# Mamba and ternary FFN block on eight cores: the tile that holds the scan's states is made bf16 instead of fp32

## The reference, cut to what matters

```python
def step(state, inp):                       # selective scan, one token
    dt_t, u_t, B_t, C_t = inp
    dA = jnp.exp(dt_t[:, :, None] * A[None])
    dBu = (dt_t * u_t)[:, :, None] * B_t[:, None, :]
    state = state * dA + dBu
    y_t = jnp.einsum('bdn,bn->bd', state, C_t)
    return (state, y_t)
...
y = (scan(x) + D[None, :, None] * x) * silu(z)
attn = (y @ _H) @ W_out.T                   # _H: Hadamard, 4096 x 4096
...
h1 = x @ ternary_quant(w1).T ; h3 = x @ ternary_quant(w3).T
ffn = (silu(h1) * h3) @ ternary_quant(w2).T
out = x_in + attn + ffn                     # x = layernorm(x_in) feeds both
```

## Time and profile before

| | us |
|---|---|
| median of 2 runs | 10670.43 (10645.05 to 10695.81) |
| the profiled execution's own time | 10478.75 |
| its span on the slowest core (core 5) | 10476.7 |
| spans of the eight cores | 10430.5 to 10476.7 |
| VectorE busy in that span | 6517.8 (62%) |
| TensorE matmuls busy | 5633.2 (54%) |
| ScalarE busy | 2399.2 (23%) |
| GpSimd busy | 1936.0 (18%) |

### The profile page before, as it was taken

One profiled execution on the slowest core, in us unless ns is written; L12 is line 12 of the kernel. 1 busy time (PEld: TensorE's weight loads), 2 busy tenths in 40 slices (PEclk: granted clock), 3 DMA queues, 4 the chain that ended last, 5 costly groups with the idle time before them and its releaser, 6 DMA issues. The chain is left out here.

```text
span 10476.7 us, 83345 instructions; the slowest of 8 cores (10430.5 to 10476.7 us)
## 1 busy us (share of the span) xinstructions
PE 5633.2 (54%) x21820; PEld 2115.9 (20%) x21820; DVE 6517.8 (62%) x7631; ACT 2399.2 (23%) x2891; POOL 1936.0 (18%) x2775
## 2 busy tenths in 40 slices
PE   4999200002999714555535555535554536555288
PEld 2444100001444201111111111111111212222033
DVE  0000757776540007888959999859998858888811
ACT  0000100000331163333323333323333212222200
POOL 0000000011111002222222222222222222222200
PEclk9999555555999956888877888878886768888599
DMA  5222698876666551111131111141111353333066
GB/s 94 59 56 60 184 262 279 237 241 179 139 136 114 131 137 33 40 40 40 40 37 37 40 40 40 40 39 38 40 40 29 107 91 102 117 114 96 24 187 192
DMA packets 830020, 1033.85 MB, mean 99 GB/s; under 512 B 186545, under 2 KB 659250, under 8 KB 803890
## 3 DMA queue, kind: packets, MB, share of 16 engines
q1 hardware_dynamic: 619826, 736.70, 24.9%
q0 software_dynamic: 209728, 291.81, 13.6%
HBM read 820.50 MB, written 274.99 MB: 105 GB/s over the span
## 5 line engine op out<-in xcount | busy, mean ns | idle before, releaser
L1208 ACT ACTIVATE p6e<-p6dl,a_sb 128x512 f32<-128x512 f32 x2048 | 1467.5, 721 | 4198.6 <-DVE p6s L1261 4174.9
L1419 PE MATMUL pA<-p6cs,identng_sb 128*128 128x512 bf16 x2048 | 941.1, 460 | 2593.7 <-DVE p6cs L1270 2593.5
L1093 POOL COPY state_sb<-p6s 128x1 f32<-128x1 f32 x2048 | 1435.7, 701 | 4162.0 <-DVE p6s L1261 4162.0
L1261 DVE TENSOR_TENSOR_SCAN p6s<-p6e,state_sb,p6db 128x512 f32<-128x512 f32 x1536 | 1972.0, 1284 | 164.5 <-DVE p6db L1250 6.4
L1270 DVE TENSOR_TENSOR p6cs<-p6s,p6cb 128x512 bf16<-128x512 f32 x2048 | 1417.8, 692 | 251.3 <-PE pA L1419 32.7
L1341 PE MATMUL pB<-xn_f,f1a 128*128 128x512 bf16 x2752 | 943.2, 475 | 21.3 <-DMA f1a<-W1Ts 20.8
L1419 PEld LDWEIGHTS pA<-p6cs,identng_sb 128*128 128x128 bf16 x2048 | 204.5, 100 | 3647.8 <-issue 3627.5
L1378 PE MATMUL pB<-f2g,f2w 128*128 128x512 bf16 x2752 | 733.4, 405 | 336.4 <-DMA f2w<-W2Ts 336.4
L1310 PE MATMUL pB<-xn_f,f1b 128*128 128x512 bf16 x2752 | 880.3, 449 | 5.0 <-DVE f1g L1230 4.9
L1250 DVE TENSOR_TENSOR p6db<-p6du,p6bb 128x512 bf16<-128x512 bf16 x2048 | 859.0, 419 | 13.4
L442 DVE TENSOR_REDUCE ln_cols<-x_t 128x1 f32<-128x2048 f32 x17 | 38.8, 2280 | 1014.1 <-DMA x_t<-XPAD 1014.1
(11 more groups left out here) (112 smaller groups left out, 4727.9 us busy)
## 6 DMA issues: line engine op xcount, KB each, us to landing
q_f<-W1P SPq DMA_DIRECT2D x86, 1024.0 KB, 10.5
q_f<-W3P SPq DMA_DIRECT2D x86, 1024.0 KB, 10.7
q_f<-W2P SPq DMA_DIRECT2D x86, 1024.0 KB, 8.6
f2w<-W2Ts SPq DMA_DIRECT2D x64, 704.0 KB, 4.8
f2w<-W2Ts SPq DMA_DIRECT2D x64, 672.0 KB, 5.1
p3st<-WIN POOLq DMA_DIRECT2D x64, 512.0 KB, 10.2
XCs<-p3xc POOLq DMA_DIRECT2D x32, 1024.0 KB, 4.4
SZGs<-p3z POOLq DMA_DIRECT2D x32, 1024.0 KB, 11.3
```

The lines of the kernel that those rows point to most:

```text
L1093: s_gc.inc(gpsimd.tensor_copy(state[:, g * NS + n:g * NS + n + 1], s_bK[k % 3][:, NB - 1:NB]))
L1208: s_ee.inc(scalar.activation(e_b[k % 3][:, :], dlt_b[g % 2][:, :], AF.Exp, scale=a_sb[:, g * NS + n:g * NS + n + 1]))
L1261: s_sc.inc(vector.tensor_tensor_scan(s_bK[k % 3][:, :], e_b[k % 3][:, :], dbu_b[k % 2][:, :], (state[:, g * NS + n:g * NS + n + 1] if cc > ...
L1419: s_im.inc(tensor.matmul(pA[:, ysl:ysl + NB], ident_ng[:, :], cs_b[k % 8][:, :], start=(n == 0), stop=(n == NS - 1)))
```

## The change

The three state tiles `s_bK` become bf16 instead of fp32, and the tiles behind them in SBUF move up, since each state tile now takes 1 KB of a partition instead of 2 KB. No call in any engine's program is changed. Compared row by row, the built programs have the same instructions in the same order and number on TensorE, VectorE, ScalarE and SyncE (the scan and the multiply keep their names, and only the type of a tile is another). On GpSimd the 2048 rows of L1093 stand where they stood, but are called CAST where they were called COPY, since source (bf16) and destination (fp32) now differ in type. The scan's output is rounded to bf16: the multiply of L1270 and the state handed to the next chunk take the rounded values.

```diff
-    s_bK = [big(f"p6s_{i}", [128, NB], F32, P6O + (11 + i) * NB * 4)
+    s_bK = [big(f"p6s_{i}", [128, NB], BF16, P6O + 11 * NB * 4 + i * NB * 2)
             for i in range(3)]
-    dtu_b = [big(f"p6du_{i}", [128, NB], BF16, P6O + 14 * NB * 4 + i * NB * 2)
-             for i in range(2)]
+    dtu_b = [big(f"p6du_{i}", [128, NB], BF16,
+                 P6O + 11 * NB * 4 + (3 + i) * NB * 2) for i in range(2)]
     dbu_b = [big(f"p6db_{i}", [128, NB], BF16,
-                 P6O + 14 * NB * 4 + (2 + i) * NB * 2) for i in range(2)]
+                 P6O + 11 * NB * 4 + (5 + i) * NB * 2) for i in range(2)]
     cs_b = [big(f"p6cs_{i}", [128, NB], BF16,
-                P6O + 14 * NB * 4 + (4 + i) * NB * 2)
+                P6O + 11 * NB * 4 + (7 + i) * NB * 2)
             for i in range(8)]
     yg_stg = [big(f"p6yg_{i}", [128, NB], BF16,
-                  P6O + 14 * NB * 4 + (12 + i) * NB * 2)
+                  P6O + 11 * NB * 4 + (15 + i) * NB * 2)
               for i in range(2)]
-    SEND = P6O + 14 * NB * 4 + 14 * NB * 2
+    SEND = P6O + 11 * NB * 4 + 17 * NB * 2
```

## The result

The changed kernel takes 10137.43 us (median of 11 runs, 9990.84 to 10331.6), the kernel before 10681.9 us (median of 10 runs, 10493.87 to 10846.26). These two medians have the ratio 0.949. The ratio 0.9536, with a 95% interval of 0.9377 to 0.9695, is that of the runs in which neither die was held back by a lower granted clock. The forecast was 10129 us and a ratio of 0.949.

What follows compares the result with a forecast made beforehand. The prediction took VectorE's own instructions in the long stage as the bound. 1984 steps saving 0.273 us each, 541.6 us, off the median 10670.4 gave 10128.8 us, ratio 0.949, with a range of 9925 to 10340 us.

Steps and rivals of the forecast that it cites:

- The bound: Long stage: VectorE's own row of instructions is the path, busy 5078.1 of 5975.0 us; a step takes 2.52 us.
- The multiply: L1270, all tiles bf16, falls from 692 to 419 ns as L1250 has; the period goes from 2.52 to 2.25 us.
- The scan: L1261, now writing bf16, stays at 1225 ns in the first chunk and 1284 in the others; bounds -0.27 and +0.55 us.
- the straight line through the plain products: VectorE products with an fp32 input cost 1.04 ns per element whatever the output type, so the scan should not change.
- The rival of a further pass: Writing bf16 after an fp32 input costs the scan a third pass: 559 us slower, 11229 us; chance 0.03.
- The cast: GpSimd's L1093, off the path, takes 0.44 us beside the shorter L1270 and costs the path nothing.
- The rival that GpSimd gets in ahead of L1250: The waiting cast takes the shared port first for 183 ns; saving only 179 us, time 10492 us; chance 0.04.
- The four slots: Slots 90, 98, 106 and 114 are bound by TensorE, which starts late after transfers; their 64 steps gain nothing.
- TensorE: Elsewhere it keeps up: at most 2.29 us per five-matmul step, about two steps later catching up in L1378; takeover rival 0.06.
- The boundary waits: Three VectorE waits for the broadcasts into `Cb` at chunk boundaries move ahead as a block and stay 288.9 us.
- The sum: Whole kernel: 1984 steps x 0.273 us = 541.6 us saved.
- The base: Saving taken off the runs' median, 10670.4 us, which lies 191.7 us above the profiled execution, unexplained by any row.

## Why the prediction was right

**The bound.** Right. The run with two of three tiles shows that every step counts for itself. One reading beside it was wrong: the 127 waits at a slot's end are less than 1 us only on average (111.6 / 127 = 0.88); the longest is 3.4 us, in the rows themselves. Nothing in the sum hangs on it.

**The multiply.** Right, and mis-sized by 6 ns: 425 instead of 419. L1250 has the form but not the position. It starts 0.08 us before its predecessor ends, while L1270 has waited for the scan. The first L1250 of a slot, which has waited too (0.10 us of idle time before it, as before L1270), takes 426 ns on average over the 128 slots, and the others take 419. The step fell by 0.267 us, not by 0.273.

**The scan.** Right: its 1284 and 1225 ns to the digit in the changed kernel, and within 4 ns in all that only laid the tile otherwise. The bounds of -0.27 and +0.55 us were wide; the straight line through the plain products was the better guide. The rival of a further pass is out.

**The cast.** Right with its 0.44 us and its price of nothing. The rival that GpSimd gets in ahead of L1250 is out: without the casts the step is the same. A 512-column cast does hold VectorE up, but at the scan, a meeting that the prediction didn't have.

**The four slots.** Right: 52 to 55 us before and after, with 10.0 us more of waiting inside them, where 9 had been forecast, and 8.0 more at their ends (11.3 to 19.4). Together that is about what 64 steps x 0.267 us would have saved.

**TensorE.** Right. In slots 0 to 87 every identity matmul started within 0.15 us of its product (core 7). The hardest case, the lower clock in the first chunk, is seen in slot 2:

```profile
4071.18 1.91 PE L1341 MATMUL pB<-xn_f,f1a 128*128 128x512 bf16 x4
4072.99 0.58 PE L1419 MATMUL pA<-p6cs,identng_sb 128*128 128x512 bf16 x1
4073.37 1.86 PE L1341 MATMUL pB<-xn_f,f1a 128*128 128x512 bf16 x4
4075.19 0.38 PE L1419 MATMUL pA<-p6cs,identng_sb 128*128 128x512 bf16 x1
```

TensorE has no idle time left there, yet the identity matmuls keep VectorE's beat of 2.20 us. So the 2.29 us that the prediction read for such a step was too high, as it suspected. In the ordinary slots of L1378 TensorE had caught up by the eleventh step at the latest; in slot 103 at the tenth, where it had been the sixth, so four steps later and not about two. The saving was full there all the same. The stage's granted clock rose from 0.78 to 0.81.

**The boundary waits.** The term "they stay 288.9 us" was off by a little: 300.1 us on core 7. Over the cores one such wait took 86 to 100 us before and 90 to 105 after, and on core 5, where the 288.9 were read, the three came to 276 afterwards, so this is spread between cores and runs.

**The sum.** 1984 steps x 0.267 us are 529.7 us. Less 11.2 at the boundaries and 1.3 in the four slots, that leaves 517.2, and the stage fell by 521.8. The terms account for it within 5 us. The 54 us missing from the whole span are 31.4 ahead of the stage, 2.5 behind it and 20 in these terms. Core by core the stage fell by 508 to 546 us.

**The base.** The median of the runs stands 191 us above the profiled execution before, and I had left that unexplained and carried it over. It came out so: 10137 measured, 10129 forecast. That the two agree within 9 us is in part luck. The runs of each kernel spread over some 350 us, the medians differ by 544.5 us, and the two profiled executions by 488. The episodes of lower clock in stages that TensorE sets are such a cause, and lie in code that the change doesn't touch. That they make up the whole gap wasn't measured, as those runs have no traces.

## What to carry to other kernels

Look for the one operand that keeps an instruction on the path from its short form, here an fp32 tile between two bf16 ones. Price it by an instruction of the same shape that already has the form, in the same position with respect to its waits, and count only the steps in which that engine is really waited for. The form went when one input's 16-bit elements weren't neighbours, which the type on a profile's row doesn't tell, and the scan showed no such form with any type that was tried (its second input was always bf16).

## What the runs showed of the hardware that was not expected

- A bf16 input that starts 2 bytes behind a multiple of 4 left the product at 425 ns; one with elements 4 bytes apart took 693.
- GpSimd's one-column copy takes 183 ns alone and ends about 0.05 us behind a VectorE product that it meets, 709 or 440 ns after its start as the product is the long or the short one. A faster VectorE instruction made GpSimd's busy time fall by 541 us.
- A 512-column cast on GpSimd lengthens a scan on VectorE from 1284 to 1443 ns, inside the scan's own duration and without a wait in any list; the scan then ends 1.074 us behind the cast, whichever its own length.
- Pairs of cores run TensorE's full stages at a granted clock of 0.82 to 0.87 for hundreds of us while the others have 1.00, and are up to 126 us later for it.
